# Delta rule's block inverse: odd chunks on exchanged array tiles, both parities in one instruction, T turned by products

## The reference, cut to what matters

```python
def step(state, inp):
    q_t, k_t, v_t, b_t, g_t = inp
    state = state * jnp.exp(g_t)[..., None, None]
    for j in range(nh):
        kj = k_t[:, j]
        corr = jnp.einsum('bhk,bhkv->bhv', kj, state)
        u = (v_t[:, j] - corr) * b_t[:, j][..., None]
        state = state + jnp.einsum('bhk,bhv->bhkv', kj, u)
    o_t = jnp.einsum('bhk,bhkv->bhv', q_t, state)
    return (state, o_t)
```

## Time and profile before

| | |
|---|---|
| median of 3 runs | 4395.57 us (4390.56 to 4404.54) |
| span of the profiled execution | 4401.2 us, from its first to its last instruction |
| TensorE matmul / weight load | 4098.5 us busy (93%) / 3392.4 us (77%) |
| VectorE / ScalarE / GpSimd | 3015.5 us (69%) / 2178.4 us (49%) / 1584.0 us (36%) |
| delta rule stage | GpSimd's work per unit recurs from some 150 to some 2460 us |
| mean granted TensorE clock | 0.974 of 2.4 GHz; 0.99 between 150 and 2000 us |

### The profile page before, as it was taken

The page is one execution under the profiler, slowest core; times in us unless marked ns, Lnnn a source line. Parts: engine busy times, 40 slices in busy tenths (PEclk is TensorE's granted clock), DMA queues, the critical chain, the costliest instruction groups (busy, mean ns, idle before and its releaser), DMA issues. The chain is left out here.

```text
span 4401.2 us, 105534 instructions
## 1 busy us (share of the span) xinstructions
PE 4098.5 (93%) x36303; PEld 3392.4 (77%) x36303; DVE 3015.5 (69%) x8155; ACT 2178.4 (49%) x5662; POOL 1584.0 (36%) x2836
## 2 busy tenths in 40 slices
PE   5699999999999999999999779879999999999979
PEld 5488888888878887878888668857777777777768
DVE  4577777777777777777777444356776776776655
ACT  3355555555555555555555234344444444444344
POOL 0466666666666666666666100000000000000010
PEclk9999999999999999999999689989999999999989
DMA  4333333333333333333333142121111111111021
GB/s 159 92 81 89 80 80 90 80 80 98 91 90 80 81 93 80 85 84 80 89 80 84 57 136 86 39 78 48 52 47 38 52 48 37 52 48 48 10 69 34
DMA packets 541045, 322.11 MB, mean 73 GB/s; under 512 B 249552, under 2 KB 498896, under 8 KB 538832
## 3 DMA queue, kind: packets, MB, share of 16 engines
q1 hardware_dynamic: 540496, 315.14, 25.3%
HBM read 230.96 MB, written 83.99 MB: 72 GB/s over the span
## 5 line engine op out<-in xcount | busy, mean ns | idle before, releaser
L950 DVE SCALAR_TENSOR_TENSOR g_conv<-g_r,g_taps,g_conv 128x511 f32<-128x511 f32 (+2 forms) x961 | 698.6, 741 | 135.0 <-ACT g_conv L833 126.5
L1997 ACT ACTIVATE a_pr<-a_pr,a_low 128x128 f32<-128x128 f32 (+3 forms) x512 | 286.5, 560 | 392.0 <-DVE a_low L2142 376.0
L837 ACT ACTIVATE g_us<-g_chn 128x128 f32<-128x128 f32 x528 | 146.2, 277 | 664.0 <-PE g_chn L632 663.3
L2297 POOL TENSOR_TENSOR a_dg<-a_const,a_fl 128x384 fp32r<-128x384 f32 x32 | 26.5, 827 | 1156.4 <-DVE a_fl L2149 1156.4
L557 PE MATMUL g_r<-g_x_hi,g_w_hi 128*128 128x512 f32 x770 | 367.0, 477 | 9.4 <-issue 7.1
L2142 DVE CUSTOM_DVE_ANT_0 a_pr<-a_sc,a_bias 128x128 f32<-128x128 f32 (+3 forms) x512 | 242.3, 486 | 192.7 <-issue 173.8
L557 PE MATMUL g_r<-g_x_hi,g_w_lo 128*128 128x512 f32 x770 | 307.1, 399 | 0.0
L557 PE MATMUL g_r<-g_x_lo,g_w_hi 128*128 128x512 f32 x770 | 305.5, 397 | 0.0
L1825 PE MATMUL a_out<-a_pt,a_v 128*128 128x512 f32 (+3 forms) x1024 | 297.2, 433 | 0.9 <-DVE a_oT L2162 0.9
L833 ACT ACTIVATE g_conv<-g_r,g_taps 128x512 f32<-128x512 f32 x321 | 220.4, 687 | 135.0 <-PE g_r L557 123.4
L1151 POOL TENSOR_TENSOR g_prod<-g_small 64x14 f32<-64x14 f32 (+6 forms) x896 | 228.5, 255 | 158.7 <-DMA g_small<-lower_d 93.4
(11 more groups left out here) (358 smaller groups left out, 11974.7 us busy)
## 6 DMA issues: line engine op xcount, KB each, us to landing
g_w_raw<-w_heads SPq DMA_DIRECT2D x66, 768.0 KB, 4.9
lower_d<-g_L SPq DMA_DIRECT2D x64, 512.0 KB, 3.3
g_T<-low_d SPq DMA_DIRECT2D x64, 512.0 KB, 5.0
g_U<-upp_d SPq DMA_DIRECT2D x64, 512.0 KB, 6.3
a_w<-w_groups SPq DMA_DIRECT2D x32, 640.0 KB, 4.6
oT_d<-g_oT SPq DMA_DIRECT2D x67, 256.0 KB, 6.3
f_oT<-oT_d SPq DMA_DIRECT2D x8, 2048.0 KB, 9.4
a_wo<-wo_b SPq DMA_DIRECT2D x32, 512.0 KB, 5.4
```

The costliest lines, as they stand in the source:

```text
L950: ins = V.scalar_tensor_tensor(out=y[:, k:L], in0=x[:, 0:L - k], scalar=tap, in1=y[:, k:L], op0=ALU.mult, op1=ALU.add)
L1997: A(pr[g % 2][:, i, 0:width(i)], pr[g % 2][:, i, 0:width(i)], ACT.Exp, scale=-1.0, bias=low[g % 2][:, i:i + 1], accum_out=tot[g % 2][:, i: ...
```

## The change

It rewrites the three levels. Chunks are taken by parity instead of by halves: even chunks write bank 0, odd chunks bank 1 of one PSUM tensor `lev`, and an odd chunk's rows of `T` lie in the other half of the partitions (`home`), so that its products use other 32x32 array tiles than those of the even chunk beside it. VectorE handles both parities in one instruction: one mask per level, four adds at the first level, two at the second, one at the third. The transposes of `U` go: at the first level `un_small` makes the turned columns as further products with `nu0`, whose first 16 columns are a constant identity; at the last level `nu_last` multiplies by the identity, into the same order as its other products. The products of the second level use 32x32 tiles instead of 64x64. `T` is loaded by three transfers instead of one, since its odd chunks change halves; they wait for the second level of the turn instead of the third. `gram` and `lower` go by parity. VectorE's order at the end of the turn changes: the first half of `bv` comes before the reduction of the squares, the last mask before the norm. `lev_mask`, `lev_add`, `lev_T` and `copy_T` are replaced by functions per level. The core of the diff:

```diff
-        lev = [ps(f"g_lev{i}", [P, HC, P]) for i in (0, 1)]
+        lev = ps("g_lev", [P, 2, HC, P])
...
+        def parity(m):
+            return m[:].rearrange("p (c e) n -> p e c n", e=2)
+        QUAD = [slice(i, i + 2 * SM) for i in range(0, P, 2 * SM)]
+        def home(i, c):
+            return i ^ 2 if c % 2 else i
...
-                sp.wait_ge(s["d_un"], NL2 * u + NL2)
+                sp.wait_ge(s["d_un"], NLV * u + NLV - 1)
                 sp.wait_ge(s["d_XT"], 32 * u + 32)
-                sp.dma_start(T[:], chunks_of("low_d")).then_inc(s["d_TU"], 16)
+                rows_T = chunks_of("low_d").rearrange("p (c e) n -> p e c n", e=2)
+                sp.dma_start(parity(T)[:, 0], rows_T[:, 0]).then_inc(s["d_TU"], 16)
+                for to, of in ((slice(0, C), slice(C, P)), (slice(C, P), slice(0, C))):
+                    sp.dma_start(parity(T)[to, 1], rows_T[of, 1]).then_inc(s["d_TU"], 16)
...
+            def nu_small(u, o):
+                for p in range(HC):
+                    for c in (2 * p, 2 * p + 1):
+                        for i, at_ in enumerate(QUAD):
+                            mm = M.matmul(lev[QUAD[home(i, c)], c % 2, p, 0:SM], Lm[o][at_, c, at_], U[o][at_, c, at_.start + SM:at_.stop], start=True, stop=True)
+            def un_small(u):
...
+                            M.matmul(lev[at_, c % 2, p, SM:2 * SM], T[h, c, at_], nu0[h, c, SM:2 * SM], start=True, stop=True)
...
+                            mm = M.matmul(lev[h, 0, p, (2 + c % 2) * SM:(3 + c % 2) * SM], nu0[h, c, :], first, start=True, stop=True)
+            def nu_mid(u, o):
...
+                            mm = M.matmul(lev[QUAD[home(i, c)], c % 2, p, 4 * SM:6 * SM], Lm[o][d, c, a], U[o][d, c, d], start=True, stop=True)
+            def un_mid(u):
...
+                            mm = M.matmul(lev[a, c % 2, p, 6 * SM:8 * SM], T[h, c, a], nu1[h, c, :], start=True, stop=True)
+            def nu_last(u, o):
...
+                        turned = M.matmul(lev[h, 0, p, 0:C], U[o][0:C, c, 0:C], ident[0:C, 0:C], start=True, stop=True)
+                        mm = M.matmul(lev[h, 1, p, C:P], Lm[o][C:P, c, 0:C], U[o][C:P, c, C:P], start=True, stop=True)
+            def un_last(u):
...
+                        mm = M.matmul(lev[0:C, e, p, 0:C], T2[h, p, :], nu2[h, p, :], start=True, stop=True)
...
                 chain_ks(u, q, 5)
                 if inverse:
-                    lev_nu(u, o, 0, 0, own)
+                    nu_small(u, o)
                 chain_u(u, par, 5)
-                if inverse:
-                    lev_nu(u, o, 0, 1, own)
...
                 chain_ks(u, q, 6)
...
+                    have_U(u, 0)
+                    have_copy(u, 0)
+                chain_u(u, par, 6)
+                if inverse:
+                    nu_mid(u, o)
                 chain_s(u, q, 6, made)
...
+                    have_mask(u, 1)
                 chain_ks(u, q, 7)
                 if inverse:
+                    un_mid(u)
                 chain_u(u, par, 7)
...
+            def copy_small(u):
+                act.wait_ge(s["d_U0"], u + 1)
...
+            def mask_last(u):
+                dve.wait_ge(s["d_nu"], NLV * u + 3)
+                V.tensor_tensor(nu2[:], lev[:, 1, :, C:P], levels[:, 2, :].unsqueeze(1).to_broadcast([P, HC, C]), ALU.mult).then_inc(s["d_nus"], 1)
...
                 chain_S(u, q, 5)
+                    add_small(u, o, (0, 2), "d_U0")
                 chain_R(u, q, 6)
+                    add_small(u, o, (1, 3), "d_U")
...
+                    add_mid(u, o)
+                if own:
+                    dve.wait_ge(s["d_rk"], u + 1)
+                    ch.link(V.tensor_tensor(bk[:], rk[:], tab[par][:, 0, :], ALU.mult))
...
+                    values(0)
                 dve.wait_ge(s["d_osq"], u + 1)
...
+                    values(1)
+                    mask_last(u)
```

More of the change, by code:

```diff
@@ L41 @@
                       ("tails", TT * (TT - 1)), ("tail_count", TT), ("pick_group", HKV * P),
-                      ("below", SM * SM), ("unit", SM * SM)):
+                      ("below", SM * SM), ("unit", SM * SM), ("first", SM)):
     CONSTS[_name] = (_at, _at + _width)
@@ L73, in constants @@
     put("levels", lev.reshape(P, len(LEVELS) * C))
+    put("first", r[:, None] % (2 * SM) == np.arange(SM)[None, :])
     put("below", np.tile(-np.tril(np.ones((SM, SM)), -1).reshape(1, -1), (P, 1)))
@@ L656, in turn, with gram @@
                 keys = lambda x: x[:].rearrange("p (c t) j -> p c (t j)", c=NC)
[L658 to L661 removed]
+                def gram(e):
+                    for p in range(HC):
+                        k = keys(kT[q])[:, 2 * p + e, :]
+                        mm = M.matmul(lev[:, e, p, :], k, k, start=True, stop=True)
                     mm.then_inc(s["d_gram"], 1)
@@ L733, in turn @@
                     spread_end(u + 1)
-                chain_s(u, q, 5, made, (0, 0) if inverse else None)
+                chain_s(u, q, 5, made, 0 if inverse else None)
                 if inverse:
-                    lev_un(u, 0, 0)
-                    have_mask(u, 0, 1)
+                    un_small(u)
                 chain_ks(u, q, 6)
-                if inverse:
-                    lev_un(u, 0, 1)
-                chain_u(u, par, 6)
                 if own:
@@ new lines, in add_small, with add_mid @@
+            def add_small(u, o, quads, sem):
+                dve.wait_ge(s["d_un"], NLV * u + 1)
+                for i in quads:
+                    to = parity(U[o])[QUAD[i], :, :, QUAD[i].start + SM:QUAD[i].stop]
+                    ins = V.tensor_tensor(to, to, lev[QUAD[i], :, :, SM:2 * SM], ALU.add)
+                ins.then_inc(s[sem], 1)
+            def add_mid(u, o):
+                dve.wait_ge(s["d_un"], NLV * u + 2)
+                for i in (0, 2):
+                    to = parity(U[o])[QUAD[i], :, :, QUAD[i + 1]]
+                    ins = V.tensor_tensor(to, to, lev[QUAD[i], :, :, 6 * SM:8 * SM], ALU.add)
+                ins.then_inc(s["d_U"], 1)
@@ L982, in chain_R, with add_last @@
+            def add_last(u, o):
+                dve.wait_ge(s["d_un"], NLV * u + 3)
+                to = parity(U[o])[0:C, :, :, C:P]
+                V.tensor_tensor(to, to, lev[0:C, :, :, 0:C], ALU.add).then_inc(s["d_U"], 1)
             def chain_R(u, q, c):
```

227 lines of the change are left out of this document (91 added, 136 removed).

## The result

The changed kernel takes **4413.23 us** (median of 7 runs, 4406.02 to 4425.15) against 4395.57: ratio 1.0044, 95% interval 1.0032 to 1.0057. That is 17.7 us slower, where 20.8 us faster was forecast; the time lies inside the range, on the wrong side. The profiled execution took 4407.28 us (span 4405.5), near the low end of its runs, so the two traces differ by only 4.3 us of span. So 13.4 of the 17.7 us between the medians do not show in this pair of traces. The seven runs of the changed kernel order themselves by TensorE's mean clock: 0.948 in the quickest (4406), 0.942 in the slowest (4425).

A forecast was written before the change was run, and what follows sets the result against it. The prediction took a ring over GpSimd, SyncE and VectorE as the bound, with 0.45 us of slack a unit. 63 x (-0.45 + 0.2) - 5 = -20.8 us from the median gave 4375 us, range 4335 to 4420.

The forecast's parts named there:

- The ring as the bound: Delta rule stage: GpSimd's inverse, SyncE's table load, GpSimd's dm and VectorE's L form a cycle, 35.06 us in one unit.
- Its signs: Profile after: L 0.12 us behind dm, TensorE's share about 90%, idle before chain_ks(5), inverse every 35.5 us.
- the sign named for a missing cover: SyncE's queue: the table landing later by as much as it is issued later would show the forecast wrong.
- I cost this at nothing: SyncE's queue: two more issues for T, 1.04 us a unit, taken as covered by 1.6 us of backlog.
- I take 0.2: T's two 64-partition transfers: price of their rate, 0.2 us a unit, within bounds 0 and 0.83.
- The estimate from the Trainium skill's SBUF — State Buffer: T's loads: by the rule that 64-partition transfers serialize, 0.54 us more a unit, no change at 4396 us.
- Rival (a): SyncE's queue behind T: ring longer by up to 0.83 us a unit, 4414 us; decides from 0.74; chance 0.13.
- TensorE's side gets 1.5 us shorter: Levels and turn's end: 3.9 us less TensorE work a unit, after added waits 1.5 us shorter.
- All that can be won: At L: the ring's slack, 0.57 - 0.12 = 0.45 us a unit, caps gains from speeding up the other side.
- the forecast's sum for loads at nothing: Whole kernel: the forecast with the price of T's loads at nothing, 4362 us.
- The last turns: After the last inverse: 3.9 us of work and 1.5 us of the last full turn, 5 us saved in all.

The follow-up runs named there:

- e7: Kernel before, with the next unit's table issued right behind the stores of the inverse instead of behind T, U and the store of oT; ratio 0.9952.
- e8: Changed kernel with eight filling transposes ahead of the wait before chain_u(6) and the table issued early; ratio 0.9812.
- e13: Kernel before, with T loaded by three transfers, each over all 128 partitions, not exchanged; ratio 1.0017.
- e2: Changed kernel with T loaded by one transfer as before, odd chunks not exchanged, so other blocks are multiplied; ratio 0.9993.
- e4: Changed kernel with eight more identity transposes ahead of the wait before chain_u(6), to fill TensorE's idle time; ratio 0.9999.
- e1: Kernel before, with T loaded by three transfers, one over 128 partitions and two over 64, not exchanged; ratio 1.0031.
- e5: Changed kernel with both eight filling transposes ahead of chain_u(6) and T by one transfer, odd chunks not exchanged; ratio 0.9951.
- e10: Kernel before, with the previous unit's qden computed in the middle of the turn instead of at its end; ratio 0.9974.
- e12: Changed kernel, table issued early, qden moved to mid-turn, chain_u(6) ahead of the waits for sums and copy, one identity product before nu_mid, no filling; ratio 0.9799.

## Why the prediction was wrong

- **The ring as the bound**: right, and shown by e7 and e8. Its signs came in part: `L` waits for `dm` more often (39 units), TensorE's share is 89%, and TensorE stands ahead of `chain_ks(5)` in 18 of 58 units instead of 4. But the inverse recurs every 35.93 us, not 35.5, and the table, issued 0.24 us later, landed 0.60 later: the sign named for a missing cover.
- **The step that failed first: "I cost this at nothing" and "I take 0.2"** for `T`'s three loads. Together they cost 0.54 us: 0.27 by three transfers in place of one, and 0.27 by the halves. The issues were covered (the table was issued only 0.24 us later), but `U`'s bytes, ahead of the table's, came later, and the backlog that I took for a cover of the issues was the very thing that got longer. That is 0.34 us more than forecast, 63 x 0.34 = 21 us. The estimate from the Trainium skill's SBUF — State Buffer ("Can I just issue two DMAs to hit both halves?"; the two rates stand in "Door 1: The DMA port swizzle"), 0.54 us, equals the sum, but e13 leaves to the 64 partitions only half of it. Rival (a) had the place right, not the price: 0.54 us is less than the 0.74 from which it was to decide, and with 0.54 its sum is 63 x 0.09 - 5 = +1 us. That its time, 4414 us, is nearly the measured one is luck: about half of the loss (e2 22 us, e4 20) is the clock, which it did not hold.
- **The second: "TensorE's side gets 1.5 us shorter".** The sizes were about right or better: levels at 4.5 us (5.1 forecast), VectorE at 3.7 (3.8), TensorE idle for 1.04 us at `chain_u(6)` (1.2); the 1.1 us ahead of `K0`'s second piece were not foreseen. What was missing is the clock, which no part of the sum and no rival held: at half clock in 256 us of the stage, TensorE's side lost 1.1 us a unit between `chain_u(6)` and `chain_s(7)`. How little was left shows in e2, where `dm` comes nearly as in the kernel before (15.24 against 15.20): `L` is 0.59 us behind it, as before (0.57), so nothing of the 0.45 us was won. The 0.34 us of the change are no sign of a shorter side, since three loads alone bring the distance to 0.26 (e1); filled (e4), it is 0.15. Measured against the forecast's 0.12, 0.215 us a unit are missing, 63 x 0.215 = 14 us in the profiled execution. With the clock cured and the table out of the way the saving is 1.0 to 1.3 us.
- **"All that can be won" is 0.45**: the period of e5, 35.32 us, is the one that the forecast had for this, in one execution; by its ratio e5 wins 22 us, where the forecast's sum for loads at nothing has 33. Its clock is not all cured (21 stretches in the stage), and `L` is still 0.27 us behind `dm`. As a reading it was wrong: about a third of the 0.45 was not TensorE's lateness but GpSimd's multiplications holding VectorE (e10).
- **The last turns** gave 1.2 us instead of 5; TensorE's clock is at half for 92 to 96 us there, in both kernels. In the profiled pair the rest closes: forecast -20.8, + 21 for the loads, + 14 for the slack that was not won, + 4 for the last turns, less 9 for `L` to the inverse (0.14 a unit, not forecast) and less 4 in later stages gives +5; measured +4.3. The further 13 us between the medians stay open: no trace here is of an execution that shows them.

## What to carry to other kernels

Where a ring over several engines and a queue sets the period, a change that saves work elsewhere and adds transfers to that queue is judged by the queue first, and by when the bytes behind them land, not by when they are issued; take the waiting link out of the ring (here a 20 KB table that only had to be issued earlier), and the saving shows. A rearrangement that packs small products together and adds a wait can save TensorE's time and cost its clock: look at the granted clock behind the packed stretch, and try full-sized work in it (here 20 us). A distance between two events of two engines is not one engine's lateness until the instructions between them have been checked for waits that no semaphore shows.

## What the runs showed of the hardware

- TensorE fell to half clock behind a stretch of 4.2 us in which it was busy for 3.66, 1.6 of it with 32x32 tiles (e12). The Trainium skill, TensorE: Matmul & The Clock Gate, "HAM oscillation — how this bites in real kernels", warns of long idle gaps; in this stretch the longest was 0.41 us, and the clock fell all the same.
- A VectorE instruction on 128x4 elements in SBUF took up to 2.2 us while GpSimd multiplied 128x512, and 0.16 us beside an idle GpSimd (e10).
- The issue of one and the same store on SyncE takes more or less time by its place: `oT`'s took 1.8 us when it came 1.5 us behind the issue of `T` (before), and 0.7 when it came 2.8 us behind it (the change; means of 58 units).
- An issue that comes earlier need not land earlier: in e13 the table was issued 0.17 us earlier than in the kernel before and landed 0.33 later, 1.06 us behind `U`.
